# Local attention in a stack of mixers: the query halves of the rotation are added on VectorE, and the four engines' work is put in a new order

## The reference, cut to what matters

```python
def attn_layer(x, Wqkv, qs, ksc, Wo):                    # 16 heads of 64, windows of 32
    q, k, v = split(x @ Wqkv)                             # 3 x 1024 columns
    q = l2norm(q) * qs;  k = l2norm(k) * ksc
    q = q * cos * scale + rotate_half(q) * sin * scale    # the rotation: a sum of two parts
    k = k * cos * inv   + rotate_half(k) * sin * inv
    out = local_attention(q, k, v)                        # each window sees itself and the one before
    return out @ Wo

def ffn_layer(x, g, bln, W1, b1, W2, b2):
    xn = layernorm(x) * g + bln
    a, gate = split(xn @ W1 + b1)
    return a * gelu(gate) @ W2 + b2
x = attn_layer(shift_tokens(x), ...) + x
x = ffn_layer(shift_tokens(x), ...) + x                   # six times
```

## Time and profile before

| | us |
|---|---|
| median of 3 runs | 6340.22 |
| the three runs | 6333.89, 6340.22, 6348.62 |
| profiled execution | 6338.8 |
| its span | 6337.0 |
| TensorE busy in the span | 4931.0 (78%) |
| ScalarE busy | 4294.6 (68%) |
| VectorE busy | 3823.0 (60%) |
| GpSimd busy | 2532.1 (40%) |

### The profile page before, as it was taken

The page is one execution under the profiler, slowest core; times in us unless marked ns, Lnnn a source line. Parts: engine busy times, 40 slices in busy tenths (PEclk is TensorE's granted clock), DMA queues, the critical chain, the costliest instruction groups (busy, mean ns, idle before and its releaser), DMA issues. The chain is left out here.

```text
span 6337.0 us, 176217 instructions
## 1 busy us (share of the span) xinstructions
PE 4931.0 (78%) x69200; PEld 3188.2 (50%) x69200; DVE 3823.0 (60%) x6000; ACT 4294.6 (68%) x8831; POOL 2532.1 (40%) x1027
## 2 busy tenths in 40 slices
PE   1000059999999999987777799999999999968779
PEld 0000026666666666653333366666666666624444
DVE  4555566666666666656555466666666666556876
ACT  4333337777777777756999767777777777648668
POOL 0000035555555555532444465555555555400000
PEclk6555579999999999996666699999999999979889
DMA  1000022222222222210000022222222222100000
GB/s 49 0 0 0 0 58 53 65 57 65 57 65 57 65 57 66 55 39 1 1 0 0 23 55 63 60 63 60 62 60 62 60 62 59 46 9 4 0 3 8
DMA packets 181325, 248.29 MB, mean 39 GB/s; under 512 B 52076, under 2 KB 80232, under 8 KB 180072
## 3 DMA queue, kind: packets, MB, share of 16 engines
q1 hardware_dynamic: 176264, 221.95, 14.1%
q10 hardware_dynamic: 4320, 15.73, 0.9%
HBM read 43.50 MB, written 5.24 MB: 8 GB/s over the span
## 5 line engine op out<-in xcount | busy, mean ns | idle before, releaser
L401 PE MATMUL PS<-arena 128*128 128x512 f32 x2304 | 1169.9, 604 | 25.1 <-ACT arena L763 17.4
L1070 POOL TENSOR_TENSOR arena<-arena 128x1024 f32<-128x1024 f32 x192 | 550.7, 2868 | 932.1 <-DVE arena L969 932.1
L1070 POOL TENSOR_TENSOR lns<-arena 128x1024 f32<-128x1024 f32 x192 | 543.1, 2829 | 650.3 <-DVE arena L969 636.9
L939 DVE TENSOR_REDUCE arena<-PS 128x16 f32<-128x1024 f32 x192 | 235.2, 1225 | 773.7 <-PE PS L428 773.7
L958 DVE TENSOR_REDUCE arena<-arena 128x32 f32<-128x2048 f32 x192 | 438.9, 2286 | 391.5 <-ACT arena L763 391.5
L1440 PE MATMUL PS<-arena 128*128 128x512 f32 x8 | 5.4, 839 | 803.4 <-DVE arena L1374 803.4
L765 ACT ACTIVATE arena<-PS 128x512 f32<-128x512 f32 x384 | 229.9, 599 | 561.1 <-PE PS L401 555.1
L1073 POOL TENSOR_TENSOR lnc<-arena 128x1024 f32<-128x1024 f32 x192 | 546.4, 2846 | 0.0
L455 PEld LDWEIGHTS PS<-arena 64*64 64x64 f32 x24576 | 473.5, 134 | 144.7 <-issue 137.2
L1073 POOL TENSOR_TENSOR arena<-arena 128x1024 f32<-128x1024 f32 x192 | 542.1, 2823 | 0.0
L762 ACT ACTIVATE arena<-PS 128x512 f32<-128x512 f32 x768 | 481.4, 627 | 65.4 <-PE PS L401 40.1
(11 more groups left out here) (261 smaller groups left out, 11251.4 us busy)
## 6 DMA issues: line engine op xcount, KB each, us to landing
arena<-arena SPq DMA_DIRECT2D x2880, 64.0 KB, 2.0
arena<-in_L_ffn_Wqkv ACTq DMA_DIRECT2D x30, 512.0 KB, 4.0
arena<-in_L_ffn_Wo SPq DMA_DIRECT2D x48, 128.0 KB, 2.8
scratch<-arena SPq DMA_DIRECT2D x4, 1024.0 KB, 4.9
arena<-scratch SPq DMA_DIRECT2D x4, 1024.0 KB, 8.1
arena<-in_L_ffn_W SPq DMA_DIRECT2D x12, 341.0 KB, 2.9
arena<-in_L_ffn_Wqkv SPq DMA_DIRECT2D x6, 512.0 KB, 4.6
arena<-in_ffn_scales SPq DMA_DIRECT2D x12, 128.0 KB, 3.1
```

The source lines that it names most:

```text
L401: pe.matmul(PS[:, QKV + bank, :], xs[uu % 2][:, par * P:(par + 1) * P], w, start=True, stop=True).then_inc(qkv_ready, 1)
L1070: pool.tensor_tensor(halves(heads(t2)), halves(heads(raws[par]))[:, :, ::-1, :], sine, ALU.mult)\
```

## The change

Three parts.

**The sum of the query halves.** A new step on VectorE, `add_rotated`, adds t2 to t1 in place over the 1024 query columns of a tile and signals `q_rotated`. TensorE then transposes the 8 query blocks once (`c < 2`); the 8 key blocks keep their two transposes each. A tile has 24 transposes where it had 32.

```diff
@@ turn_qk
                 pe.wait_ge(turned_copied, nth(g, TURN_PER, n))
-                if c % 2 == 0:
-                    pe.wait_ge(t2_ready, nth(g, 2 * TILES, 2 * tt + c // 2) + 3)
-                    pe.wait_ge(t1_ready, nth(g, 2 * TILES, 2 * tt + c // 2) + 3)
+                if c == 0:
+                    pe.wait_ge(q_rotated, nth(g, TILES, tt))
+                if c == 2:
+                    pe.wait_ge(t2_ready, nth(g, 2 * TILES, 2 * tt + 1) + 3)
+                    pe.wait_ge(t1_ready, nth(g, 2 * TILES, 2 * tt + 1) + 3)
                 for j in range(4):
...
+                    if c < 2:
+                        last = pe.transpose(o, t1[:, cols], ident[:])
+                        continue
                     pe.matmul(o, t1[:, cols], ident[:], start=True, stop=False, is_transpose=True)
                     last = pe.matmul(o, t2[:, cols], ident[:], start=False, stop=True, is_transpose=True)
@@ fa_vector
+            def add_rotated(g, tt):
+                t1, t2 = t1s[tt % 2], t2s[tt % 2]
+                dve.wait_ge(t2_ready, nth(g, 2 * TILES, 2 * tt) + 3)
+                dve.wait_ge(t1_ready, nth(g, 2 * TILES, 2 * tt) + 3)
+                dve.tensor_tensor(t1[:, 0:INNER], t1[:, 0:INNER], t2[:, 0:INNER], ALU.add).then_inc(q_rotated, 1)
```

```diff
@@ fa_vector body
                     if feed and tt == 2:
                         gated(g, 0, 1)
+                    if ahead:
+                        softmax_shift(g, tt + 1)
                     if feed and tt == 3:
-                        add_down(g, b, 0, 0)
                         add_down(g, b, 1, 1)
                     if feed and tt == 2:
-                        gated(g, 1, 0)
-                        gated(g, 2, 1)
+                        gated(g, 1, 1)
                     if feed and tt == 0:
                         normalise(run, b, 1)
-                    if ahead:
-                        softmax_shift(g, tt + 1)
+                    if nearer:
+                        add_rotated(g, tt + 2)
+                    if feed and tt == 2:
+                        gated(g, 2, 1)
+                    if further:
+                        unit_length(g, tt + 3)
                     if tt % 2 == 1:
                         add_stream(g, b, tt // 2)
-                    if further:
-                        unit_length(g, tt + 3)
@@ fa_scalar body
+                    exps(g, tt)
+                    if ahead:
+                        copy_turned(g, tt + 1, 0)
                     if further:
                         copy_qkv(g, tt + 3, 0, PROJECTION_BANK[tt][0], True)
                     if ahead:
-                        copy_turned(g, tt + 1, 0)
-                    exps(g, tt)
+                        copy_turned(g, tt + 1, 1)
```

```diff
-                           .then_inc(hd_max if t else b1_max, 1)
-                    dve.wait_ge(b1_max, nth(b, PAIRS8, u))
-                    dve.wait_ge(hd_max, nth(g, PAIRS8, u))
+                           .then_inc(b1_max, 1)
+                    dve.wait_ge(b1_max, nth(b, 2 * PAIRS8, 2 * u + 1))
```

More of the change, by code:

```diff
@@ L532, in body @@
                 heads(g, 0, 1, final)
-                chunk_read(g, 3, 3)
+                if feed:
+                    mean_read(g)
+                else:
+                    chunk_read(g, 3, 2)
                 qkv(run, b, 3, 4, 0)
-                scores(g, 1, 1)
                 if feed:
@@ L563, in body @@
                     gate(run, b, 0, 0)
-                turn_probs(g, 1, final)
                 scores(g, 2, 0)
+                scores(g, 2, 1)
                 if feed:
@@ L576, in body @@
                 heads(g, 1, 1, final)
-                project(run, b, 0, 0)
                 if not final:
@@ L583, in body @@
                     qkv(run, b, 4, 4, 1)
-                scores(g, 2, 1)
-                project(run, b, 0, 1)
+                project(run, b, 0, 0)
                 if not final:
@@ L591, in body @@
                     qkv(run, b, 4, 5, 0)
+                project(run, b, 0, 1)
+                turn_qk(g, 3, 0)
                 if not final:
@@ L608, in body @@
                     qkv(run, b, 5, 3, 0)
+                turn_probs(g, 2, final)
+                scores(g, 3, 0)
+                scores(g, 3, 1)
                 if feed:
@@ L692, in body @@
                     else:
-                        chunk_read(g, 6, 3)
+                        chunk_read(g, 6, 1)
                     qkv(run, b, 6, 5, 1)
+                project(run, b, 1, 1)
             first = call * DEPTH
@@ L861, in body @@
                     if ahead:
-                        copy_turned(g, tt + 1, 0)
-                    exps(g, tt)
+                        copy_turned(g, tt + 1, 1)
+                    if feed and tt == 0:
+                        shift(g, b)
                     if further:
@@ L867, in body @@
                         load_projection(l, 0)
-                    if feed and tt == 0:
-                        shift(g, b)
                     if ahead:
-                        copy_turned(g, tt + 1, 1)
+                        copy_turned(g, tt + 1, 2)
                     if further:
@@ L890, in body @@
                         copy_gate(g, 1, 1)
+                    if further:
+                        rnorm(g, tt + 3)
+                    if feed and tt == 1:
                         copy_gate(g, 2, 0)
@@ L893, in body @@
                         inverse_deviation(g, 1)
-                    if tt % 2 == 0 and not final:
-                        enter(g, b, (tt + 4) // 2)
                     copy_heads(g, tt, 0)
@@ L899, in body @@
                         copy_qkv(g, tt + 3, 4, PROJECTION_BANK[tt][4], True)
-                        rnorm(g, tt + 3)
+                    if tt % 2 == 0 and not final:
+                        enter(g, b, (tt + 4) // 2)
+                    if further:
                         copy_qkv(g, tt + 3, 5, PROJECTION_BANK[tt][5], True)
@@ L1007, in body @@
                     ahead = not (final and tt + 1 >= TILES)
+                    nearer = not (final and tt + 2 >= TILES)
                     further = not (final and tt + 3 >= TILES)
@@ L1010, in body @@
                     if feed and tt == 0:
-                        centre(g, 1)
+                        centre(g, 0)
+                    if feed and tt == 3:
+                        add_down(g, b, 0, 1)
                     if further:
```

125 lines of the change are left out of this document (56 added, 69 removed).

## The result

The changed kernel takes **6251.59 us** (median of 4 runs, 6238.35 to 6268.55) against 6344.42 us of the kernel before beside it (4 runs, 6333.89 to 6348.75): a ratio of 0.9858, 95% interval 0.9827 to 0.9888. It gains 93 us where 152 were forecast. The profiled execution took 6260.15 us; its span is 6258.4 us.

The account below looks back on a forecast made before the run. TensorE was taken as the bound, busy 75.9 of 78.2 us a body, ScalarE not far behind. 6338.8 less 147 (3.2 us, 46 bodies) less 4 (attn_b1) gave 6188 us; own range 6150 to 6230, 8 in 10 range 6090 to 6275.

Parts of the forecast that it names:

- rival (b): ScalarE: copies queue behind `exps`, first in a step; if `softmax_shift` is late, gain halved, 6261 us; chance 0.16.
- Transposes: TensorE, each tile: eight transposes fewer save 0.87 us, 167 us over 192 tiles.
- Addition: VectorE, before `unit_length`: 1.22 us each with GpSimd idle; VectorE busy some 235 us longer.
- rival (c): VectorE's addition meets a busy GpSimd and takes 3.0 to 3.4 us; slower, 6381 us; chance 0.07.
- Steps of the body: The loop body's four steps take 17.5, 19.85, 17.8 and 19.85 us, 75.0 where it had 78.2.
- second pair: Step 0: `shift` goes ahead of this pair on ScalarE, so the fourth projection waits 0.7 us for its bank.
- copy of part 4: Step 2: the last projection uses this copy's bank and starts at 15.9 instead of 14.7, 1.2 us lost.
- rival (a): Loop body: the new order hides half of ScalarE's idle time, 5.2 us a body, 6096 us; chance 0.13.
- 3.2 us a body, 46 times: 147 us: Loop: each of 46 bodies counted as full falls from 78.2 to 75.0 us.
- The order takes away about as much waiting as it brings: Loop body: transposes alone are 3.5 of the 3.2 us saved; the new order's waits about cancel.
- attn_b1: VectorE behind the two maxima: one wait less saves 0 to 4 us over 64 times; 4 taken.
- (d): TensorE: single transposes no faster than pairs, so 3.5 us a body come back, 6349 us; chance 0.03.

Follow-up runs that it names:

- e2: The changed kernel without the addition, with all 32 transposes and the new order kept: 6295.09 us, ratio 0.9915 to the kernel before.
- e1: The kernel before with only the addition (behind `norms`) and the single transposes, in the old order: 6429.93 us, ratio 1.0122 to the kernel before.
- e7: The old order with the single transposes and the addition moved behind `softmax_shift`: 6489.88 us, ratio 1.0235 to the kernel before.

## Why the prediction was partly right

The time is in the range, the direction is right, and 61% of the gain came. But it lies outside the forecast's own range (6150 to 6230), and the wider one takes it in only for the sake of rival (b), at 6261 us, whose mechanism cost 18 us at most (below) and not the 74 that it was priced at: that part is luck. Step by step:

- **Transposes: right.** From the first of four singles to the next instruction are 0.44 to 0.49 us, 0.87 to 0.90 for the eight of two transposes a block: half, block for block.
- **Addition: right in the loop, wrong at a call's start.** Median 1.22 us as taken; VectorE is busy 272.6 us longer, not 235; the additions are 243 of it. At a call's start they take 3.3 to 3.4 us and TensorE waits 6.66 us, twice: 13 of the 23 us more up to the first mean and between the calls. The prediction left the prologue out ("the first body has no feed-forward"), and there rival (c) is what happened.
- **Steps of the body: right where nothing interrupts.** Forecast 17.5, 19.85, 17.8, 19.85; measured 17.38, 19.58, 17.44, 19.51. Steps 1 and 3 have no idle time left. The waits named are there; the timeline of TensorE in the quiet body has

```profile
4801.75 1.12 PE L402 MATMUL PS<-arena 128*128 128x512 f32 x2 [0.40 <-ACT arena L760]
4803.22 1.12 PE L486 MATMUL PS<-XN,mean_w 128*128 128x512 f32 x2 [0.34 <-ACT arena L760]
...
4812.18 1.12 PE L402 MATMUL PS<-arena 128*128 128x512 f32 x2 [0.58 <-DVE XN L996]
...
4840.39 1.88 PE L434 MATMUL PS<-arena 64*32 64x64 f32 x128 [0.37 <-ACT PS L794]
...
4848.51 1.13 PE L402 MATMUL PS<-arena 128*128 128x512 f32 x2 [0.83 <-ACT arena L762]
```

  against forecasts of 0.7 (second pair), 0.6 (third), 0.7 (`normalise`), 0.5 (mask) and 1.2 (copy of part 4). The 0.3 for the addition didn't come. Each was a little too high, and the quiet body is 1.0 us shorter than forecast, some of rival (a).
- **"3.2 us a body, 46 times: 147 us": the step that failed.** It took the quiet body for the mean one, and 46 bodies for full where 44 are. Before, quiet and full mean are 78.1 and 79.1; after, 73.95 and 77.2. The term for idle time without a releaser and for the clock behind it is missing, and it is 2.3 us a body. The row was on the page before, 13.4 us at the heads, and the prediction doesn't mention it. The two stretches that aren't full gave 14 us, most of it by the clock in one of them, which nothing in the prediction foresaw.
- **"The order takes away about as much waiting as it brings": wrong.** e2 shows 2.0 us a body from the order alone in quiet bodies, and e1 nothing from the transposes alone. The sum charged the two parts separately; they only pay together.
- **attn_b1: too high.** The gap behind the maxima shrank from 0.10 to 0.04 us, as said,

```profile
5953.91 1.01 DVE L2016 TENSOR_REDUCE arena<-arena 128x2 f32<-128x256 f32 x2
5954.96 0.17 DVE L2019 TENSOR_SCALAR arena<-arena 128x4 f32<-128x4 f32 x1
```

  but from the first to the last unit the stage takes 264.3 us instead of 265.0: 0.7 us, not 4, inside the 0 to 4 given.
- **Rivals.** (b) shows in one place, for another reason than `softmax_shift`. At each of the eight turns of the loops ScalarE stands between its branch and `exps` for 2.5 to 3.5 us, with nothing to wait for; every copy queues behind, and TensorE waits 1.8 to 2.75 us for the turned block, 18 us in all. ScalarE's and TensorE's timelines:

```profile
4028.64 1.06 ACT L789 ACTIVATE arena<-arena 128x1024 f32<-128x1024 f32 x1 [3.13 <-issue]
```
```profile
4030.42 0.30 PE L421 MATMUL PS<-ident,lnc 128*128 128x128 f32 x1 [2.75 <-ACT arena L784]
```

  The kernel before has such stops of ScalarE too (2.2 to 2.5 us), and TensorE waits of up to 1.6 us behind them, so only the difference is the change's. (c) holds in the prologue and in the old order only. (d) is out.

## What to carry to other kernels

On TensorE a dense run of hundreds of short matmuls has a second limit beside its own pace: look at idle time that nothing releases, count what is left of the group behind it, and if that number repeats from run to run it is tied to the code's position, which some 64 idle transposes ahead of the code can test. Before multiplying a body's saving by the number of bodies, compare the quiet body with the mean one, and treat a call's first and last tiles apart. An edit that frees the bound and a new order may each be worth little alone, so measure both halves before crediting either.

## What the runs showed of the hardware

- The time of this kernel hangs on where its TensorE code stands modulo 256 instructions: the mean body is 76.5 us at a shift of 0 and of 256, 75.4 to 75.7 at 128, 76.8 at 192.
- TensorE's gaps in short matmuls end 1.2 to 1.6 us after the end of a 16 KB packet of the instruction queue, in all 333 gaps of 1 us or more.
- The granted clock fell to half 19 times in the change's 44 full bodies, 17 of them behind gaps of 1.2 to 2.6 us (0.50 in the stretch behind 4191.75) and two behind waits of 2.53 and 2.75 us for ScalarE, and the clock's part of the loss was as large as the gaps' own. Such a stop doesn't always lower it: in the 44 full bodies before the change, with 14 stops of 1.0 to 1.7 us, it stood at 1.00 throughout, and e7, with 1.83 us twice in each body, has it low in 4 bodies of 44. What decides between them isn't shown.
- VectorE's addition of 128x1024 elements took 1.22 us with GpSimd idle and 3.3 to 3.4 beside it, with both inputs in SBUF.
